# Attention without transposes: scores by rows for the maxima, by columns for exp, and part of the splitting on GpSimd

## The reference

```python
# layer 0: layer norm, a rank-8 scan, a low-rank FFN, then a gated FFN with a Walsh-Hadamard transform
# layer 1, attention (x is 2 x 1024 x 512, 16 heads of 32):
qkv = x @ W_qkv.T + b_qkv
q, k, v = jnp.split(qkv, 3, axis=-1)          # each reshaped to b, l, h, e
scores = jnp.einsum('bqhe,bkhe->bhqk', q, k) * scale
scores = jnp.where(causal[None, None], scores, -jnp.inf)
attn = jax.nn.softmax(scores, axis=-1)
out = jnp.einsum('bhqk,bkhe->bqhe', attn, v)
out = out.reshape(b, l, d) @ W_out.T + b_out
# layer 1, FFN: silu(x @ w_gate) * (x @ w_up), the two largest of each four kept, @ w_down
```

## Time and profile before

| | us |
|---|---|
| median of 3 runs | 1736.83 (1734.71 to 1737.45) |
| the profiled execution, its own time | 1735.48 |
| its span in the trace | 1733.6 |
| busy in the span: PE / DVE / ACT / POOL | 1675.1 / 1039.5 / 710.8 / 286.4 |
| granted TensorE clock, mean | 0.989 |

### The profile page before, as it was taken

How to read it: one execution, slowest core, us unless ns; L and a number is a source line. 1 busy time by engine, 2 the same in 40 slices (tenths; PEclk the granted TensorE clock), 3 DMA queues, 4 the chain that set the end, 5 groups by cost and what they waited for, 6 DMA issues and landing times. The chain is left out here.

```text
span 1733.6 us, 22683 instructions
## 1 busy us (share of the span) xinstructions
PE 1675.1 (97%) x8316; PEld 1337.6 (77%) x8316; DVE 1039.5 (60%) x1795; ACT 710.8 (41%) x1271; POOL 286.4 (17%) x281
## 2 busy tenths in 40 slices
PE   5999999999999999989999999989999999999998
PEld 3677888788788877767777777768888888888887
DVE  4321365564623454348999999965655555555785
ACT  4421322232213332238999999962222222222221
POOL 4201210310310102110000000023244031033330
PEclk9999999999999999999999999999999999999999
DMA  7200210100101037942555445523010010012243
GB/s 292 96 12 1 61 49 19 55 31 23 57 7 37 25 113 249 290 192 65 141 146 133 128 132 151 139 68 135 0 52 25 1 49 25 0 49 71 76 140 128
DMA packets 69662, 150.11 MB, mean 87 GB/s; under 512 B 9577, under 2 KB 18409, under 8 KB 68018
## 3 DMA queue, kind: packets, MB, share of 16 engines
q1 hardware_dynamic: 69554, 148.70, 27.5%
HBM read 102.13 MB, written 46.53 MB: 86 GB/s over the span
## 5 line engine op out<-in xcount | busy, mean ns | idle before, releaser
L1566 DVE TENSOR_TENSOR pt_lo<-p_turn,pt_hi 128x512 fp32r<-128x512 f32 (+3 forms) x384 | 200.3, 548 | 8.1 <-ACT pt_hi L1540 7.9
L1559 DVE TENSOR_REDUCE row_top<-p_score 128x1 f32<-128x128 f32 (+7 forms) x256 | 188.9, 748 | 16.3 <-PE p_score L1493 16.2
L1532 ACT ACTIVATE prob<-p_score,row_top 128x128 f32<-128x128 f32 (+7 forms) x256 | 185.8, 740 | 12.9 <-DVE row_top L1559 11.7
L1540 ACT ACTIVATE pt_hi<-p_turn 128x512 fp32r<-128x512 f32 (+3 forms) x384 | 182.0, 491 | 9.6 <-PE p_turn L1504 4.7
L1504 PE MATMUL p_turn<-ident,prob 128*128 128x128 f32 x1152 | 183.1, 277 | 1.1 <-DVE pt_lo L1566 0.8
L1025 DVE TENSOR_TENSOR hid<-hid,p_up 128x512 f32<-128x512 f32 x64 | 44.0, 687 | 217.1 <-PE p_up L490 201.4
L1895 DVE TENSOR_TENSOR e_hid<-e_hid,e_p_up 128x512 f32<-128x512 f32 x64 | 44.0, 687 | 196.5 <-PE e_p_up L1790 196.5
L1504 PEld LDWEIGHTS p_turn<-ident,prob 128*128 128x128 f32 x1152 | 130.3, 142 | 22.6 <-issue 8.8
L1519 PE MATMUL p_o<-pt_hi,v 128*65 128x512 f32 (+3 forms) x384 | 141.7, 376 | 2.8
L1491 PE MATMUL p_score<-stack 128*128 128x512 f32 (+3 forms) x384 | 128.5, 389 | 8.6 <-PEq L55 3.5
L772 ACT ACTIVATE hid<-p_gate 128x512 f32<-128x512 f32 x64 | 38.3, 599 | 218.3 <-PE p_gate L490 218.2
(11 more groups left out here) (269 smaller groups left out, 3930.6 us busy)
## 6 DMA issues: line engine op xcount, KB each, us to landing
stack<-qk_parked SPq DMA_DIRECT2D x256, 128.0 KB, 3.9
raw<-in_wgu SPq DMA_DIRECT2D x64, 256.0 KB, 2.7
qk_parked<-qk SPq DMA_DIRECT2D x16, 1024.0 KB, 4.0
v_parked<-v_out SPq DMA_DIRECT2D x16, 520.0 KB, 6.0
v<-v_parked SPq DMA_DIRECT2D x8, 1040.0 KB, 9.9
o_parked<-o_both SPq DMA_DIRECT2D x64, 128.0 KB
res<-in_x SPq DMA_DIRECT2D x8, 512.0 KB
rot<-in_w2t SPq DMA_DIRECT2D x4, 1024.0 KB, 7.4
```

Source lines behind the costliest of these rows:

```text
L1532: act.activation(row_at(h, r, 0, width_of(r)), p_score[:, r % 2, 0:width_of(r)], ACT.Exp, bias=top[:, r:r + 1]).then_inc(exped, 1)
L1540: act.activation(pt_hi[:, (BL * h + j) % PT, c0:W], p_turn[:, (BL * h + j) % TB, c0:W], ACT.Copy).then_inc(rounded, 1)
L1559: dve.tensor_reduce(top[:, r:r + 1], p_score[:, r % 2, 0:width_of(r)], AX_X, ALU.max, negate=True).then_inc(topped, 1)
L1566: dve.tensor_tensor(pt_lo[:, slot, c0:W], p_turn[:, (BL * h + j) % TB, c0:W], pt_hi[:, slot, c0:W].bitcast(F32), ALU.subtract).then_inc(sp ...
```

## The change

Scores are now made twice. The first time by rows as before, but over 96 partitions: the product of the two lo parts is left out, and a stack is loaded in 6 DMAs instead of 16 (load_part), into one of three places. These scores serve the maxima alone, and the maximum frees their place. Each row's negated maxima, one per partition, are then moved by a DMA (place) into one partition: the 97th of the queries' side of the stack, whose counterpart on the keys' side holds ones. The second time (turned_score) keys are the stationary side, so that scores come out already turned, with 97 partitions and thus less the maximum; where a block crosses the diagonal a mask product follows. ScalarE takes exp of a whole block from PSUM into prob, which now has five slots of 512 columns, then rounds from SBUF into pt_hi; VectorE subtracts with both inputs in SBUF. Blocks 1, 4, 6 and 8 (OWN) are rounded and subtracted on GpSimd instead (divide). The ones are set by GpSimd, in project_qkv and at the start of attention. SyncE has an order of its own in the table. Of ORDER, only the lists of GpSimd and SyncE are shown here:

```diff
-STACKS = 16 * 16
-
-
-def load_stack(sp, stack, qk_dram, it, n, stacked):
-
-    here = qk_dram[4 * it + n]
-    for a in range(2):
-        for what in range(2):
-            r = 2 * E * what + E * a
-            for block in range(4):
-                half = block // 2 if what == 0 else block % 2
-                sp.dma_start(stack[E * block:E * block + E, n % 2, a, what].bitcast(F32),
-                             here[half, r:r + E, :]).then_inc(stacked, 16)
+STACKS = 16 * 6
+
+
+def load_stack(sp, slot, qk_dram, pair, stacked):
+
+    for what in range(2):
+        load_part(sp, slot, qk_dram, pair, what, stacked)
+
+
+def load_part(sp, slot, qk_dram, pair, what, stacked):
+    r = 2 * E * what
+    for block in range(3):
+        half = block // 2 if what == 0 else block % 2
+        sp.dma_start(slot[E * block:E * block + E, :, what].bitcast(F32),
+                     qk_dram[pair][half, r:r + 2 * E, :].rearrange("(a e) n -> e a n", a=2)).then_inc(stacked, 16)
...
+            pool.wait_ge(wv_split, KD)
+            for n in range(2):
+                pool.memset(stack[3 * E:3 * E + 1, n, :, 1].bitcast(F32), 1.0).then_inc(keys_set, 1)
+                pool.wait_ge(keys_set, n + 1)
...
+    PB = 5
     PT = 6
+    K3 = 3 * E
...
-    AHEAD, BEHIND = 2, 1
+    AHEAD = 2
+    OWN = (1, 4, 6, 8)
     ORDER = {
...
+        "gpsimd": [("divide", 4, 0), ("divide", 6, 0), ("divide", 8, 0), ("divide", 1, 1)],
+        "sync": [("place", 4, 1), ("store", 0, 0), ("values", 0, 0), ("place", 5, 1), ("place", 6, 1), ("place", 7, 1),
+                 ("stack", 2, 0), ("place", 0, 2), ("place", 1, 2), ("place", 2, 2), ("place", 3, 2), ("store", 1, 0)],
...
-        prob = sb("prob", [P, 2, ROWS * (ROWS + 1) // 2 * P])
-        top = sb("row_top", [P, ROWS])
+        third = sb("stack_third", [P, 2, 2, S], F32R)
+        prob = sb("prob", [P, PB, W])
+        top = sb("row_top", [P, 2, ROWS], F32R)
...
+            def place(h, r):
+                sp.wait_ge(topped, ROWS * h + r + 1)
+                if r % QB == 0:
+                    wait(sp, placed[r // QB], 16 * QB * h)
+                sp.dma_start(slot_of(h)[K3:K3 + 1, h % 2, 0, r * P:(r + 1) * P].bitcast(F32),
+                             top[:, h % 2, r:r + 1].bitcast(F32)).then_inc(placed[r // QB], 16)
...
-            def turn(it, h, j):
+            def turned_score(h, j):
                 g, kb, c0 = block_of(j)
                 if kb == 0:
-                    pe.wait_ge(exped, ROWS * (HB * it + h) + QB * (g + 1))
-                wait(pe, split, BL * (HB * it + h) + j - TB + 1)
-                for i in range(c0 // P, QB):
-                    mm = pe.transpose(p_turn[:, (BL * h + j) % TB, i * P:(i + 1) * P],
-                                      row_at(h, QB * g + i, kb * P, (kb + 1) * P), ident[:, :])
+                    pe.wait_ge(placed[g], 16 * QB * (h + 1))
+                if (h, j) == (4, 0):
+                    pe.wait_ge(ones_set, 1)
+                wait(pe, exped, BL * h + j - TB + 1)
+                both = slot_of(h)[0:K3 + 1, h % 2]
+                to = p_turn[:, (BL * h + j) % TB]
+                mm = pe.matmul(to[:, c0:W], both[:, 1, kb * P:(kb + 1) * P], both[:, 0, g * W + c0:(g + 1) * W], start=True,
+                               stop=kb < QB * g)
+                if kb >= QB * g:
+                    mm = pe.matmul(to[:, c0:c0 + P], mask[:, 0], mask[:, 1], start=False, stop=True)
...
-            def exp(it, h, r):
-                b, pr, a = place_of(h)
-                act.wait_ge(topped, ROWS * (HB * it + h) + r + 1)
-                wait(act, turned, BL * (HB * it + h - 2) + (r + 1 if r < QB else QB + r + 1))
-                act.activation(row_at(h, r, 0, width_of(r)), p_score[:, r % 2, 0:width_of(r)], ACT.Exp,
-                               bias=top[:, r:r + 1]).then_inc(exped, 1)
-            def round_block(it, h, j):
+            def exp(h, j):
                 g, kb, c0 = block_of(j)
-                act.wait_ge(turned, BL * (HB * it + h) + j + 1)
-                wait(act, weighted, BL * (HB * it + h) + j - PT + 1)
-                act.activation(pt_hi[:, (BL * h + j) % PT, c0:W], p_turn[:, (BL * h + j) % TB, c0:W],
-                               ACT.Copy).then_inc(rounded, 1)
-            def read_o(it, h, g):
-                act.wait_ge(weighted, BL * (HB * it + h) + (BL if g else QB))
-                if (it, h, g) == (0, 0, 0):
+                n = BL * h + j
+                act.wait_ge(turned, n + 1)
+                wait_split(act, n - PB)
+                act.activation(prob[:, n % PB, c0:W], p_turn[:, n % TB, c0:W], ACT.Exp).then_inc(exped, 1)
+            def round_block(h, j):
+                g, kb, c0 = block_of(j)
+                n = BL * h + j
+                act.wait_ge(exped, n + 1)
+                wait(act, weighted, n - PT + 1)
+                act.activation(pt_hi[:, n % PT, c0:W], prob[:, n % PB, c0:W], ACT.Copy).then_inc(rounded, 1)
...
-                dve.wait_ge(rounded, BL * (HB * it + h) + j + 1)
-                dve.tensor_tensor(pt_lo[:, slot, c0:W], p_turn[:, (BL * h + j) % TB, c0:W], pt_hi[:, slot, c0:W].bitcast(F32),
+                n = BL * h + j
+                dve.wait_ge(rounded, n + 1 - owned(n))
+                dve.tensor_tensor(pt_lo[:, n % PT, c0:W], prob[:, n % PB, c0:W], pt_hi[:, n % PT, c0:W].bitcast(F32),
...
+        @block.gpsimd
+        def _(pool):
+            def divide(h, j):
+                g, kb, c0 = block_of(j)
+                n = BL * h + j
+                pool.wait_ge(exped, n + 1)
+                wait(pool, weighted, n - PT + 1)
+                pool.tensor_scalar(pt_hi[:, n % PT, c0:W], prob[:, n % PB, c0:W], 1.0, 0.0, ALU.mult, ALU.add)\
+                    .then_inc(own_rounded, 1)
+                pool.wait_ge(own_rounded, owned(n))
+                pool.tensor_tensor(pt_lo[:, n % PT, c0:W], prob[:, n % PB, c0:W], pt_hi[:, n % PT, c0:W].bitcast(F32),
+                                   ALU.subtract).then_inc(own_split, 1)
+            pool.memset(third[K3:K3 + 1, :, 1].bitcast(F32), 1.0).then_inc(ones_set, 1)
+            pool.wait_ge(ones_set, 1)
+            run({"divide": divide}, ORDER["gpsimd"])
```

More of the change, by code:

```diff
@@ L1549, in read_o @@
[L1549 to L1551 removed]
+                i = (G * h + g) % OS
+                wait(act, o_stored[i], 32 * ((G * h + g) // OS))
+                act.activation(o_both[:, i], p_o[0:VC, :], ACT.Copy).then_inc(o_read, 1)
+            run({"exp": exp, "round": round_block, "read_o": read_o}, ORDER["scalar"])
         @block.vector
```

170 lines of the change are left out of this document (85 added, 85 removed).

## The result

The changed kernel takes **1764.7 us** (median of 4 runs, 1760.36 to 1765.55), the kernel before 1737.14 (4 runs, 1734.71 to 1742.11): ratio 1.015, 95% interval 1.0122 to 1.0178. The forecast was 1746, the range 1698 to 1768. The profiled execution has a span of 1763.2 us against 1733.6, 29.6 more.

The account below looks back on a forecast made before the run. TensorE, VectorE and ScalarE run close to full, TensorE fullest with 11.0 of 11.65 us a head; attention stage +13.2 and projection -4.0 make +9.2 on 1735.5, 1744.7, and the median's 1.35 more gives 1746 us, range 1698 to 1768.

Parts of the forecast that it names:

- rival B: Attention heads: VectorE and GpSimd exclude each other for the whole instruction; 12.85 us a head, 1766 us; chance 0.06.
- rival C: SyncE's queue: maxima's places queue behind stack parts and values and bound the head; 13.1 us a head, 1774 us; chance 0.05.
- Work of each engine: Attention head after the change: TensorE 10.1 us, ScalarE 8.2 to 9.3, VectorE 8.7, GpSimd 7.4.
- Is GpSimd there when VectorE wants to subtract?: Walk through one steady attention head: VectorE 8.7 us own work, about 2.7 blocked, 1.0 idle; 12.2 us against 11.65.
- The bounds, 10.7 to 12.85: Period of a head: 10.7 us if VectorE and GpSimd never meet, 12.85 if each of five meetings costs the whole instruction.
- Rival A: Attention heads: faster, as VectorE's subtractions fall into GpSimd's pauses; 1699.5 or 1721 us; chance 0.38.
- never met: Rival A's case that VectorE's subtractions never meet GpSimd's instructions: 10.7 us a head, 1699.5 us; chance 0.15 near 1700.
- half the loss: Rival A's case with half the loss from VectorE and GpSimd meeting: 11.4 us a head, 1721 us; chance 0.23.
- Places of the maxima: Eight new DMAs a head on SyncE's queue: 3.5 us for issue and 2.5 of landing, covered with 0.5 in hand.
- Stage ends: Attention stage's start and last heads: 18.1 + 31 x period, at 12.2 us a head 396.3 us, +13.2 us.
- Projection stage: Smaller stack loads let the mask land sooner, closing TensorE's gap of 2.65 us: -4.0 us, bounds 0 and -4.35.
- a granted clock below 1.00 in the stage: Sign that the forecast is wrong: TensorE's clock drops in the attention stage, with 2 us of pauses a head; no size given.

Follow-up runs that it names:

- Run 6: Changed kernel with value loads in three parts, one a head, and GpSimd's reading instructions replaced by four memsets a block, those blocks' parts left out: 1726.98 us.
- run 5: Changed kernel with value loads behind row 7's placing, cut into three parts, one a head, and the next stage's tiles four heads later: 1731.75 us, ratio 0.9975.
- run 4: Kernel before with only the smaller stack loads, 6 DMAs a pair and scores over 96 partitions: 1731.37 us.
- run 2: Changed kernel with the value loads issued from ScalarE's queue instead of SyncE's, behind the first read of p_o: 1751.92 us.
- run 12: Changed kernel with stack parts behind row 4's placing, values as one quarter a head, next stage's tiles one a head: 1777.39 us, ratio 1.0236.

## Why the prediction was right or wrong

The sign was right, and the time lies in the range, near its upper end; it lies 9 us outside the forecast's own range of 1738 to 1756. The mechanism that the forecast put first was not the one that cost the time. That the time still lies in the range is luck: the range reaches up to 1768 for rival B (1766), whose head of 12.85 us did not come, it leaves out rival C (1774, chance 0.05), whose mechanism did, and two errors of the forecast partly cancelled. Of its signs, reads 12.0 to 12.4 us apart, subtractions of 512 columns well over 0.9 us, GpSimd's over 1.3 and VectorE the fullest engine, none came: between 800 and 1140 us the subtractions of 512 columns mean 862 and 1297 ns, and TensorE is the fullest. The sign that it gave for C, TensorE waiting for the DMA of row_top, did.

- **Work of each engine.** TensorE 10.1 us, exp at the cheaper of its two prices (487 ns a piece, as the rounding), maxima unchanged: borne out as far as the trace tells. A head without a value load at 10.96 has 0.86 us over TensorE's sum.
- **"Is GpSimd there when VectorE wants to subtract?"** This walk is the first step that failed. It gave 2.7 us blocked and 1.0 idle, 12.2 us a head. Measured, the blocked time is 1.6 us (703 less 502 ns, eight times) and the period 10.96, shorter than before, where I expected it longer by 0.55. The trace says which part was too dear. There are nearly the five meetings a head that the forecast reckoned with, 4.6: 148 of the 256 subtractions start while an instruction of GpSimd runs. But only 0.49 us of that instruction is left on the mean, and a met subtraction is 0.36 us longer, where the walk's 2.7 us make 0.54 for each of five. That is 1.1 of the 1.2 us that the period was forecast too long. (What the forecast called GpSimd's subtractions in rows 9 are its additions.) Run 6 prices the lot at 0.55 us an undisturbed head, and at 4.8 us for the kernel, one run against run 5's median. The bounds, 10.7 to 12.85, held it. Rival A was nearest: its 10.7, "never met", for the undisturbed heads of 10.96, its 11.4, "half the loss", for the mean of the 25 heads without a value load, 11.29; but the two engines do meet.
- **"Places of the maxima. Covered, with 0.5 in hand."** The second step that failed, and the one that set the result. I took 2.5 us of landing from one DMA at the start of the kernel with nothing beside it, and checked row 7's placing against the stack parts only. The value load stands ahead of rows 5 to 7 in SyncE's order; I had it in rival C, at a chance of 0.05, and argued it away with the stack parts' place. There are six such loads in the loop, not seven, and each costs 6.5 us against a head of before: +39. C's mechanism was right for the value loads, and its time, 1774, was 9 us too high, since it spread the loss over all heads.
- **Stage ends.** 31 x 12.2 + 18.1 gave 396.3; measured 414.7, the miss of 18.4 us being nearly all of the 18.7 between 1746 and 1764.7. The errors had opposite signs. Of the 31 distances the first 29 are the steady stretch: six heads 5.85 us too short in the forecast (+35), the 23 others, 11.33 on the mean, 0.87 too long (-20). The stage's ends, forecast at 18.1 + 2 x 12.2 = 42.5, took 45.8 (+3): the last head takes 11.7 where I had 8.
- **Projection stage, -4.0.** Right: the stage starts 3.7 us earlier, the window of 8 us is full at clock 1.00, and run 4 shows the effect alone (4.8 us).
- **Rival B**, the whole instruction excluded. By the Trainium skill, SBUF — State Buffer, "SBUF: two separate sides", the subtraction should have waited out GpSimd's; a head of 12.85 was to follow. Plain heads of 10.96 rule that time out, but not the exclusion, and on that the trace agrees with the page. Of the 57 subtractions of 512 columns that start while GpSimd's instruction runs, 56 end 0.54 to 0.56 us after it ends, whether 0.2 or 0.7 us of it was left; those of 384 and 128 columns end 0.42 and 0.14 us after it (medians). So VectorE stands until GpSimd's instruction is through, and what was too dear was how much of it is left when they meet. (12.85 doesn't follow from the forecast's own prices: five meetings at 1.29 instead of 1.1 would make 12.2 into 13.15.)
- **A term that was only named**: "a granted clock below 1.00 in the stage". It is 0.93 from 800 to 1140 us, and behind the 5.84 us of idle before 1001.69 it is 0.50, the lower of TensorE's two levels (1.2 GHz), from 1001.69 to 1007: starts of equal products lie 0.43 us apart there instead of 0.23. TensorE's pauses cost again as it resumes; the forecast had no term for it.

## What to carry to other kernels

A DMA of 512 bytes that an engine will wait for inside a loop must be priced by where it stands among the large transfers, not by its size: take its landing time from a place of the trace with the same traffic, and read every transfer that is issued ahead of it in each kind of iteration, the rare ones above all. Here one rare megabyte in six heads of 32 turned a gain of 0.7 us an undisturbed head into a loss of 1.5%. Moving it three steps and cutting it in three brought the kernel to 0.25% under the one before, and no further, since 11 of 31 heads still take 12 to 15 us. Look also at how many parts a DMA updates its semaphore with as it lands, and whether a few parts lag. And when a walk through a schedule rests on many small estimates that all err to one side, its result is a bound rather than a middle.

## What the runs showed of the hardware that was not expected

- A 4-byte gather from 128 partitions lands in 1.9 us at best and 9.6 at worst with a megabyte issued 2.6 us ahead. Issuing that megabyte from another engine's queue (run 2) leaves heads of 13.7 to 17.8 us. In run 12 a gather takes 5.3 us with a bulk transfer issued 0.5 us **behind** it; but fourteen of its updates have come after 3.1 us, and the next two, at 988.03 and 988.56, come as the store issued ahead of it ends (updates at 987.40, 987.72 and 988.31), so the transfer behind it need not be the cause.
- Four memsets of GpSimd a block leave VectorE's subtraction at its undisturbed 501 ns, reading instructions of the same total length raise it to 688 (runs 5 and 6). A subtraction that starts inside a reading instruction of GpSimd ends a fixed time after it, 0.55 us for 512 columns, in 56 of 57 cases; the 30 that GpSimd's instruction starts beside later keep their 0.68 us.
- The output stores don't spread over the DMA engines. In the trace's packet records of the kernel before, 260 packets of 2 KB, the length of a stored row, run between 1004.2 and 1015.1 us in exactly two chains, one packet behind the other at 84 ns; over the stage two such packets at once is the usual count. The changed kernel shows the same. The Trainium skill, DMA: Bandwidth & Descriptors, "Why a DMA increments its semaphore by 16 and not by 1", says that a transfer uses the largest number of engines up to 16 that divides the outermost dimension on both sides; the store's target has 2 there, and the rows agree with that; so do the semaphores: for the two DMAs of a store the trace has five updates (two about 1 us after the issue, three later), where two placings have 32. Two of the 16 engines thus carry all stores beside their share of everything else. In the changed kernel's long head the two stores' last updates come at 991.95 and 995.85, the packets of the value load (8320 bytes) run about fourteen at a time until 993.5, two at a time from 995.5 to 998.5 and one at a time to 1000.5, and then come the load's last two updates and the placings' last six. In run 12 the last packets of the stack parts (4 KB, some 0.3 us each, about two at a time, after 989) come from about as many. A placing is done only when all its parts are. That two of sixteen parts are late, and that TensorE waits for them, is read from the trace. That row 0's placing seems to land before row 7's is no objection: rows 0 to 3 have a semaphore of their own, and 16 of their 64 updates are enough for the first count. That the stores are what makes the two parts late is argued from the order of these times; no store was cut so that it spreads, and what that would be worth stays open.
